# Cross-attention: how four row maxima reach the stacked queries, in a fused transformer block on one core

## The reference

```python
Q = (query @ Wq.T).reshape(B, T_q, N_HEADS, D_HEAD)
K = (context @ Wk.T).reshape(B, T_c, N_HEADS, D_HEAD)
V = (context @ Wv.T).reshape(B, T_c, N_HEADS, D_HEAD)
scores = jnp.einsum('bqhd,bkhd->bhqk', Q, K) / scale
attn = jax.nn.softmax(scores, axis=-1)
out = jnp.einsum('bhqk,bkhd->bqhd', attn, V).reshape(B, T_q, D)
return out @ Wo.T
```

## Time and profile before

| | |
|---|---|
| median of 3 runs | 1725.7 us (1724.34 to 1726.32) |
| span of the profiled execution | 1727.4 us |
| mean granted TensorE clock | 0.974 |
| TensorE (PE) busy | 1628.6 us, 94% |
| VectorE (DVE) busy | 1171.3 us, 68% |
| ScalarE (ACT) busy | 767.5 us, 44% |
| GpSimd (POOL) busy | 471.1 us, 27% |
| row product L915 | 32 times, 377 ns each |
| diagonal L664 | 32 times, 692 ns each |
| clearing of the key rows L339 | once, 6.92 us |

### The profile page before, as it was taken

The page is one execution under the profiler, slowest core; times in us unless marked ns, Lnnn a source line. Parts: engine busy times, 40 slices in busy tenths (PEclk is TensorE's granted clock), DMA queues, the critical chain, the costliest instruction groups (busy, mean ns, idle before and its releaser), DMA issues. The chain is left out here.

```text
span 1727.4 us, 39816 instructions
## 1 busy us (share of the span) xinstructions
PE 1628.6 (94%) x17264; PEld 1111.9 (64%) x17264; DVE 1171.3 (68%) x1400; ACT 767.5 (44%) x973; POOL 471.1 (27%) x412
## 2 busy tenths in 40 slices
PE   6999999999999999999999999896669999999998
PEld 4666666666666766666666666674447777777775
DVE  5678567457657757656766757557787767666766
ACT  5354336344444444435434533545445444344441
POOL 2323322232123123212222237632025411101133
PEclk9999999999999999999999999997879999999999
DMA  6544243334234233242233225460048655555544
GB/s 246 124 110 111 60 116 87 62 88 122 47 87 110 60 87 87 52 111 72 67 82 95 74 59 138 121 232 2 2 138 263 214 188 180 196 174 186 180 129 121
DMA packets 102151, 202.04 MB, mean 117 GB/s; under 512 B 25739, under 2 KB 25739, under 8 KB 101850
## 3 DMA queue, kind: packets, MB, share of 16 engines
q1 hardware_dynamic: 91258, 169.49, 34.1%
q0 software_dynamic: 10720, 30.02, 6.3%
HBM read 127.36 MB, written 18.90 MB: 85 GB/s over the span
## 5 line engine op out<-in xcount | busy, mean ns | idle before, releaser
L656 DVE TENSOR_REDUCE mx<-sc 128x4 f32<-128x2048 f32 x128 | 293.2, 2290 | 67.0 <-PE sc L900 66.4
L861 PE MATMUL proj<-w_hi,ctx 128*128 128x256 f16 x2048 | 273.7, 278 | 12.8 <-ACT ctx L441 12.6
L489 ACT ACTIVATE stage_w<-sc 128x1024 f32<-128x1024 f32 x256 | 248.2, 1024 | 70.8 <-PE sc L935 70.2
L875 PE MATMUL proj<-ctx,w_hi 128*128 128x512 f16 x1024 | 253.6, 380 | 0.0
L861 PEld LDWEIGHTS proj<-w_hi,ctx 128*128 128x128 f16 x2048 | 193.0, 99 | 64.6 <-issue 40.4
L452 ACT ACTIVATE stage_w<-proj 128x512 f32<-128x512 f32 x128 | 76.4, 597 | 340.8 <-PE proj L861 340.8
L383 POOL TENSOR_TENSOR acc_g<-stage_w 128x1024 f32<-128x1024 f32 x31 | 74.0, 2389 | 477.0 <-ACT stage_w L489 476.9
L678 DVE TENSOR_TENSOR acc_v<-acc_v,stage_w 128x1024 f32<-128x1024 f32 x93 | 131.9, 1418 | 87.1 <-ACT stage_w L489 84.3
L616 DVE SCALAR_TENSOR_TENSOR k_lo<-proj,k_hi 128x512 f16<-128x512 f32 x128 | 88.0, 687 | 118.6 <-ACT k_hi L461 117.7
L1166 DVE SCALAR_TENSOR_TENSOR w_lo<-stage_w,w_hi 128x2048 f16<-128x2048 f32 x64 | 144.8, 2293 | 34.2 <-ACT w_hi L1160 34.2
L875 PEld LDWEIGHTS proj<-ctx,w_hi 128*128 128x128 f16 x1024 | 90.1, 98 | 116.5 <-issue 25.1
(11 more groups left out here) (354 smaller groups left out, 2488.8 us busy)
## 6 DMA issues: line engine op xcount, KB each, us to landing
stage_w<-in_w SPq DMA_DIRECT2D x64, 1024.0 KB, 5.9
ctx_stage<-in_ctxT SPq DMA_DIRECT2D x64, 512.0 KB, 4.6
stage_w<-k_hi SPq DMA_DIRECT2D x256, 128.0 KB, 2.4
stage_w<-k_lo SPq DMA_DIRECT2D x128, 128.0 KB, 2.4
wq_f<-in_wiT POOLq DMA_DIRECT2D x24, 256.0 KB, 4.4
xg<-xbuf POOLq DMA_DIRECT2D x28, 176.0 KB, 4.4
obuf<-o_sb POOLq DMA_DIRECT2D x28, 176.0 KB, 3.5
xbuf<-final SPq DMA_DIRECT2D x17, 256.0 KB
```

The lines of the kernel that those rows point to most:

```text
L489: act.activation(probs[:, u % 4, :], unit_scores(u), ACT.Exp, scale=1.0 / sqrt(HD)).then_inc(e_ready, 1)
L656: dve.tensor_reduce(mx[:, :, kb], sc[:, :, :], AX.X, ALU.max).then_inc(m_read, 1)
L861: last = pe.matmul(out, x_part[:, kb, e, col:col + P], w_part[:, 2, e, wv], start=term == 0 and e == 0, stop=term == 2 and e == EC - 1)
L875: last = pe.matmul(proj[at % 2][:, :], w_part[:, 1, e, P * (g % G):P * (g % G) + P], x_part[:, kb, e, :], start=term == 0 and e == 0, stop ...
```

## The change

The four negated maxima of a query go as f16 into columns 96 to 99 of a tile `nm_cols` of 128 x 128 that is zero elsewhere (cleared once, on VectorE). One product with `nm_cols` as weights and the f16 identity as moving operand turns the tile: `misc[:, 0:128]` then has head j's maxima in row 96 + j. The array is used at full width, with no tile position. `set_row` copies the four rows, each four times over, into rows 96 to 99 of the queries of all four heads. So that head j takes row 96 + j alone, the stacked keys have one-hot rows there: GpSimd multiplies `ks[96:128]` for each head j, after the clearing, in place with column 96 + j of the identity. QKM goes from 97 to 100. `diag` and the product that makes it are gone; the semaphore `diag_ready` is now `nm_ready`. VectorE's step counts are no longer started from a computed base.

```diff
-QKM = QK + 1
+QKM = QK + GH
@@
-        nm = sb("nm", [P, GH], f32)
-        diag = sb("diag", [P, GH, T], f16)
+        nm_cols = sb("nm_cols", [P, P], f16)
@@ gpsimd
                 gp.memset(ks[QK:P, :, :], 1.0).then_inc(rows_set, 1)
+                gp.wait_ge(rows_set, 1)
+                for j in range(GH):
+                    gp.tensor_scalar(ks[QK:P, j, :], ks[QK:P, j, :], ident[QK:P, QK + j:QK + j + 1], 0.0,
+                                     ALU.mult, ALU.add).then_inc(rows_set, 1)
@@ scalar, set_row
                     act.activation(qs[QK:QKM, 4 * g:4 * g + 4, :],
-                                   misc[QK:QKM, :].rearrange("p (j t) -> p j t", j=GH), ACT.Copy).then_inc(row_set, 1)
+                                   misc[QK:QKM, 0:T].unsqueeze(1).to_broadcast([GH, GH, T]), ACT.Copy).then_inc(row_set, 1)
@@ vector
-                def maxima_to_diag(b, g, steps):
+                def negate_maxima(b, g):
                     dve.wait_ge(m_read, 16 * b + 4 * g + KB)
-                    steps.did(dve.tensor_reduce(nm[:, :], mx[:, :, :], AX.X, ALU.max, negate=True))
-                    steps.wait()
                     if not (isinstance(b, int) and b == 0 and g == 0):
                         dve.wait_ge(row_ready, 4 * b + g)
-                    dve.tensor_tensor(diag[:, :, :], nm[:, :].unsqueeze(2).to_broadcast([P, GH, T]),
-                                      ident16[:, :].unsqueeze(1).to_broadcast([P, GH, T]),
-                                      ALU.mult).then_inc(diag_ready, 1)
+                    dve.tensor_reduce(nm_cols[:, QK:QKM], mx[:, :, :], AX.X, ALU.max, negate=True).then_inc(nm_ready, 1)
@@
+                steps.did(dve.memset(nm_cols[:, :], 0.0))
                 for s in range(4):
                     split_ctx(0, s)
@@ tensor, maxima_to_row
-                    pe.wait_ge(diag_ready, 4 * b + g + 1)
+                    pe.wait_ge(nm_ready, 4 * b + g + 1)
@@
-                    pe.matmul(misc[QK:QKM, :], ones16[:, 0:1], diag[:, :, :].rearrange("p j t -> p (j t)"),
-                              start=True, stop=True, tile_position=(0, QK)).then_inc(row_ready, 1)
+                    pe.matmul(misc[:, 0:T], nm_cols[:, :], ident16[:, :], start=True, stop=True).then_inc(row_ready, 1)
@@
-                pe.wait_ge(rows_set, 1)
+                pe.wait_ge(rows_set, 1 + GH)
```

More of the change, by code:

```diff
@@ L186, in cross_attention @@
         m_read = sem("m_read")
-        diag_ready = sem("diag_ready")
+        nm_ready = sem("nm_ready")
         row_ready = sem("row_ready")
@@ L751, in body @@
                                 dve.tensor_scalar(var[:, 0:B - 1], mv[:, 0:B - 1, 1], EPS, None, ALU.add).then_inc(var_ready, 1)
-                        maxima_to_diag(b, g, steps)
+                        negate_maxima(b, g)
                         if last and g == 2:
@@ L813, in _ @@
                 body(0, False, steps)
-                FIRST_STEPS = steps.n
-                PER = 2 * G
                 weight_steps = Steps(dve, wq_step, 1)
                 for b in range(1, B - 1):
-                    loop_steps = Steps(dve, v_step, FIRST_STEPS + PER * (b - 1))
-                    body(b, False, loop_steps)
-                    assert loop_steps.n == PER
+                    body(b, False, steps)
                 dve.wait_ge(wmax_moved, 32)
@@ L826, in _ @@
                 dve.reciprocal(wq_inv[:, :], wscale[:, :]).then_inc(wq_scaled, 1)
-                last_steps = Steps(dve, v_step, FIRST_STEPS + PER * (B - 2))
-                body(B - 1, True, last_steps)
-                finish_group(B - 1, 3, last_steps)
+                body(B - 1, True, steps)
+                finish_group(B - 1, 3, steps)
             @block.tensor
```

## The result

The changed kernel takes 1713.7 us (median of 4 runs, 1710.67 to 1715.65) against 1725.0 us for the kernel before beside it (median of 4, 1721.54 to 1726.32). The ratio is 0.9933 with an interval of 0.9916 to 0.995: 11.3 us faster, between 8.6 and 14.5. A second series of 6 runs gave 0.9933 again. Among the experiments one execution, of late_sum, took 2766.1 us at a mean granted clock of 0.557; it has no profile, its cause is not known, and it is left out of what is said of that run. The forecast was 1718.3 us, the range 1712.5 to 1724.5. The direction is right and the time in the range; the gain was put too low, at 7.4 us. The profiled execution has a span of 1708.7 us, 18.7 less than before, and this difference is larger than that of the medians, which has to be explained too.

The account below looks back on a forecast made before the run. TensorE's issue bounds the cross-attention groups (133.0 of 135 us busy in a middle batch). Slots -10.3, last group -0.8, start +3.7 sum to -7.4 us: 1725.7 to 1718.3 us, range 1712.5 to 1724.5.

Parts of the forecast that it names:

- The slot: Row product on TensorE: 0.056 us in place of 0.40, saving 0.344 in each of 30 ordinary groups, 10.3 us.
- rival (b): Row product's weight loads are exposed: slot 0.25 us, saving only 0.15 a group, time 1724.1 us; chance 0.07.
- (e): Row product's slot stays near 0.40 us because the gap comes from the wait, not the tile: 1728.6 us; chance 0.05.
- VectorE, ScalarE, the 100 rows: VectorE's lost 0.69 us worth nothing in 31 groups; ScalarE's copy 0.59 to 0.60 us; scores over 100 rows cost nothing.
- Batch 2: Group 0's first scores wait 3.55 us for a transfer of the keys; that wait grows by what the slot gives.
- The last group: Without the diagonal the last group's scores come 0.8 us earlier; what is late next is ScalarE.
- The start: GpSimd's four key-row scalings, 2.0 us each, delay VectorE's first weight remainder and so TensorE: 3.7 us lost.
- (a): Start costs nothing: scalings do not hold VectorE's operands or end before 11.2 us; 1714.6 us; chance 0.17.
- (c): GpSimd's scalings much dearer than their slope; slower from 5.6 us each, 1760 us at 7.8 ns an element; chance 0.04.
- With the two engines taking turns: At the start GpSimd's scalings and VectorE's remainders alternate, so the weight remainder ends at 19.7 us in place of 15.93.
- 3p: Start delay formula, 3p - 2.3 us with p the length of a scaling: 3.7 us for p = 2.0.
- 3 us less: Last group: a shorter idle stretch may keep TensorE's clock up, 1715 us; chance 0.03, given together with (a).

Follow-up runs that it names:

- late_sum: Changed kernel with VectorE's last partial sum of the third group moved behind the first maximum of the fourth; 1699.1 us, ratio 0.9846 to the kernel before.
- the two pairs: Profiles of the kernel before and the changed kernel: the first pair, and both unchanged once more (1723.9 and 1712.3 us); spans 18.7 and 11.7 us less.
- full_ones: Kernel before with 128 columns of ones as full-width weights of the row product, no tile position, still 512 columns; 1715.4 us.
- narrow_turn: Changed kernel with only the 32 columns from 96 on as weights, at the old tile position; 1717.5 us.
- spare_product: Changed kernel with an unread 0.69 us VectorE product ahead of the reduction in every group; 1710.9 us.
- first pair: First profiled executions of the kernel before and the changed kernel, both as they stand; the changed one's span is 1708.7 us, 18.7 less.
- before_again: Kernel before, unchanged, one more profiled execution; 1723.9 us.
- the pair without the wait: Kernel before and changed kernel, both with VectorE's last partial sum of the third group moved behind the fourth's first maximum; 1706.2 and 1699.1 us.
- original pair: Kernel before against changed kernel, without the moved sum; gains of 11.3 and 12.7 us by the medians.
- late_scaling: Changed kernel with GpSimd's four scalings held until VectorE has formed all eight first context remainders; 1710.1 us, ratio 0.9913.

## Why the prediction was right or wrong

**The slot: right.** Predicted 0.056 us in place of 0.40, saving 0.344; measured 0.056 and, by the distances, 0.36. Over the 28 ordinary distances that is 10.1 us; the two pairs show 9.2 and 10.0, where the forecast had 10.3 over 30 groups. The loads are hidden, so rival (b) is out, and (e) too. The sentence that the slot is over its columns because of the one-column weights' load was right as well, and full_ones and narrow_turn give it its size: 0.20 us for a change of tile form and back. Where the tile is narrow its load comes after 0.42 us without a load (narrow_turn, as in the earlier trace rows); at full width it runs ahead under the products. The Trainium skill's page "TensorE: Matmul & The Clock Gate", section "The mechanism", has weight loads overlap running products only where the row group differs; here full-height loads overlap (the load at 500.69, under products whose slots run to 500.90), and the measurement decides. The same section also lets TensorE pull a load ahead when it goes to the background weight buffer, and with that sentence the trace agrees.

**VectorE, ScalarE, the 100 rows: right.** spare_product shows the 0.69 us to be worth nothing in the 28 groups of batches 0 to 6. The four-row copy takes 0.59 us (L478, 32 times), the scores 1.06.

**Batch 2: not to be told.** The distance that holds the transfer wait is 39.0 us in the mean of five profiles of the kernel before and its variants and 39.0 in the mean of nine of the changed kernel and its own; that is what absorbing the slot would give. But single executions lie between 36.3 and 41.7, which would hide 0.36 us either way. This scatter and the falls are of the size of the 5 to 9 us between the fastest and the slowest run of one kernel in a series.

**The last group: right for its own steps.** Predicted was that the scores come 0.8 us earlier and that ScalarE is late next. From the start of `denominators` to the scores it was 1111.41 - 1108.77 = 2.64 us before (that row of the old timeline starts at 1108.77) and is 1095.27 - 1093.43 = 1.84: 0.80. The wait for the reduction is down to 0.39 and ScalarE's copy starts at 1094.58, the end of its evacuations. Not foreseen was that VectorE's 0.69 us in the group before also decides, 15 us later, which of two sums goes first. I had written that in 31 groups VectorE "goes on with work that waits for others, so in 31 groups this is worth nothing on the path". In the third group of batch 7 it is worth 1.36 us, but only against executions of the kernel before in which the tie fell the other way.

**The start: mechanism and price right, the order wrong.** A scaling is 1.97 us (predicted 2.0, from two rows with one slope), the two engines hold each other back, and rivals (a) and (c) are out. The wait was to end at 19 to 20 us, or at 16 by (a), and ended at 17.63. The failed step is "With the two engines taking turns". In the trace the second scaling was ready at 11.55 but waited until VectorE had done both remainders, 13.6 or so, and took 3.88 us for it; only then was the weight remainder held by it. So one scaling less lies ahead of the weight remainder, and the formula with 2p in place of 3p gives 2p - 2.3 = 1.6 us; the wait ends 17.63 - 15.98 = 1.65 us late. Up to the first row product the loss comes to 2.2 us in the first pair and 1.6 in the second, and this part is a matter of the execution: from 19.38 us on six products take 0.66 us in the first profile of the kernel before and 1.23 in before_again, at half the pace, which puts its first row product at 55.94 in place of 55.36. The changed kernel is at 57.57 or 57.58 either way; in its first profile TensorE waits 0.28 us at 26.47 for ScalarE (L455), which stands behind a wait for VectorE's statistics (L497), and in the other two it arrives later and waits 0.04 us or not at all. So 1.6 to 2.3 us in all, where 3.7 was forecast. The Trainium skill's page "SBUF — State Buffer", section "Who interferes with whom", says that issue order decides who blocks and, of VectorE's modes with two ports, that the first to issue has the shared ports for its whole instruction while the other fully blocks. That the loser blocks agrees (3.88 us against 1.97). That the first to issue goes first does not: the scaling had been issued at 11.55, VectorE's second remainder behind its first, and the remainder went ahead.

**The clock: the miss that matters.** The sum with measured terms is -28 x 0.36 - 1.0 + (1.6 to 2.3), about -9; the pair without the wait gives 7 to 8. The original pair gives 11 to 13. The remainder of 2 to 4 us is of the size of the rarer falls, but it is argued and not shown: the intervals of the two pairs overlap. I had not looked at the falls: the waits of TensorE were read as 2.0 us a batch, and the low clock behind some of them was in the same profile, worth 1.65 us each. So the forecast of 7.4 us fell short twice the same way, by 1.4 to 2.1 us at the start, and by what is left. For the last group I did name the clock, "3 us less", with "I see no reason for either". In the first pair it did stay up (2.65 us behind the last row product), in the second it fell in both kernels and nothing was gained; of the nine profiles of the changed kernel and its variants it stayed up in that one alone.

**Against the profile, not the medians.** Of the first pair's 18.7 us some 9 belong to the slots, the start and the last group as the edit makes them; the rest is clock falls, the tie and what else this pair of executions happened to differ in. Had I read the gain off the two spans, I would have put it two thirds above the 11.3 us of the medians.

## What to carry to other kernels

A small product with a narrow tile at a position of its own between full-width products cost 0.20 us more than its columns here: on the engine that sets the time, shape it like its neighbours. Work given to GpSimd "far from its deadline" isn't free if it reads SBUF while VectorE runs two-input instructions for the critical engine; put it where VectorE reads PSUM or idles (2.45 us here), and move VectorE's own sums from where they meet GpSimd's (14 us here, falls of the clock included). And take two profiles of a kernel before explaining a difference of a few microseconds: ties of 0.03 us and clock falls of 1.65 us came out differently in two executions of the same program.

## What the runs showed of the hardware

- A narrow weight tile at position (0, 96) among full-width ones costs 0.19 to 0.20 us in all: 0.09 in front and 0.10 behind, whether it has 1 column (kernel before, against full_ones) or 32 (narrow_turn, against the changed kernel).
- A GpSimd tensor-scalar over 32 x 2048 f16 takes 1.97 us alone (late_scaling) and 3.9 to 4.9 beside VectorE's two-input instructions (changed kernel); one that waits can be passed by the next VectorE instruction too (ready at 11.55, VectorE's next began at 12.46 and kept its 1.21 us).
- A wait of 1.9 us of TensorE was followed by some 3 us at the 1.2 GHz level in some batches and not in others of the same execution; in the 18 batches 1 to 6 of the three profiles without the wait there was no such stretch.
- Two sums, on VectorE and GpSimd, that start within 0.03 us of each other: VectorE's took 1.21 us in one execution of the kernel before and 3.42 in the other.
